# Attention's mixing matmuls in pairs of 33 columns on the two halves of TensorE's array, and three of four low halves on GpSimd

## The chip, the cores and the metric

The kernel runs on one core of a Trainium2 chip. The metric is the device time of one launch in microseconds (us). Matmuls run on TensorE (PE in the rows; PEld is its weight loads), elementwise work on VectorE (DVE), ScalarE (ACT) and GpSimd (POOL), and SyncE (SP) issues most DMAs. TensorE's granted clock has two levels, 1.2 and 2.4 GHz; 1.00 in a row is 2.4 GHz throughout.

## The reference

A decoder block with four gated parts, each added to the residual `x` (4 x 512 x 512): attention over a context, a ternary mixture of experts, a cross attention with 16 heads over 1024 keys, and an expert layer. The change lies in the third:

```python
Q = query @ Wq.T + bq                      # 4 x 512 x 512, 16 heads of 32
K = key_value @ Wk.T + bk                  # 4 x 1024 x 512
V = key_value @ Wv.T + bv
scores = jnp.einsum('bhsd,bhtd->bhst', Q, K) * scale
attn = jax.nn.softmax(scores, axis=-1)
ctx = jnp.einsum('bhst,bhtd->bhsd', attn, V)
x = x + jnp.tanh(g_xattn[1]) * (ctx @ Wo.T + bo)
```

## The kernel before, in words

All values are 32-bit in the reference; the kernel splits each matmul operand into a bf16 high half and a bf16 rest (the low half), and adds the products. The program is a row of phases: `context_phase`, `readout_phase`, `router_phase`, `mixture_phase`, `query_phase`, `attention_phase`, `output_phase`, `expert_phase`. Each engine has its own instruction list, written out by hand in order; semaphores tie them together.

`attention_phase` handles batch after batch (B = 4), in each 16 heads (h), in each four quarters of the 1024 keys (u). One (b, h, u) is a *step*, 256 in all. The scores stand transposed, 128 keys by 512 queries, two blocks (i = 0, 1) a step. TensorE does in the loop of a step (`batch`):

- `max_scores` (L1846): two full matmuls for the row maxima of the step 28 steps ahead (EARLY), into one of two `psM` buffers (`wait_free` waits until what lay there two places before has been used);
- `scores` (L1865): two matmuls for the step 4 ahead (AHEAD), into `psE`;
- `mix` (L1876): for each i the exponentials' high half `upper` (the upper 16 bits of each 32-bit word of `t_e`) and their low half (`t_low`) by the values, four matmuls of 96 columns (VW = 3 x 32: values high, values low, 32 columns of ones for the softmax sums), all into `psO[0:96]`, summed over u.

The other engines:

- ScalarE: `exponentials` (L1740), two per step for 4 steps ahead; `copy_out` (L1754) of `psO` to `ost` after each head; `max_copy` (L1748).
- VectorE: `halves` (L1786), the low half of an odd quarter, 128 x 1024 elements, 3 steps ahead; then `maximum` (L1778), the reduction of `psM`, 28 steps ahead. It also splits the output bias (`split_bias`, batch 1, heads 1 to 5) and inverts the sums (L1808, batch 3, head 5).
- GpSimd: `halves` (L1697) of the even quarters (`LO_ON_POOL = (0, 2)`, L1519), 4 ahead; before each it waits until VectorE has done its earlier ones (`lo_dve`). Once in 16 steps `max_parts` (L1707 to L1713) cuts the maxima of the next four heads into three bf16 parts, at step 5 of 16.
- At step 9 of 16 TensorE transposes these parts (`max_transpose`, L1854). The transpose takes one place in the ring of two `psM` buffers, so the maximum scores right behind it need the reduction of the step before, not of two steps before.
- SyncE: one DMA per head stores `ost` (L1674), and the loads of the next batch's keys, values (L1243) and queries.

The stage's order is thus fixed by the lists; 16 steps (four heads) make one *group*, from one transpose to the next. `output_phase` then loads the mixed values, divides and projects: 12 full matmuls (L2084) and one of 3 rows for the bias (L2087, the matmul of `bones` and `brows`) per tile. `query_phase` sets the ones in `kst` and `vst` (L1336, L1338).

Of the kernel before, what the change touches and what calls it, by code (L numbers as in the profile page):

```python
# [17 lines left out]
VW = 3 * HD  # L18
# [1212 lines left out]
KV_LOADS = 7  # L1231


def load_keys_values(sp, b, g, keys_dram, values_dram, kst, vst, kv_loaded):
# [8 lines left out]
    sp.dma_start(vst[:, g, :, 0:2 * P], v_v[bb, g].rearrange("o p c n -> p (o c) n")).then_inc(kv_loaded[g], 16)  # L1243
# [16 lines left out]
def query_phase(nc, place, gates, mixture_dram, w32, w_loaded, bq, queries_dram, ident, xres, woT, kst, vst, ones_set,  # L1260
# [6 lines left out]
    with ExitStack() as c:  # L1267
# [43 lines left out]
        with nc.Block() as block:  # L1311
            @block.gpsimd
            def _(pool):
# [18 lines left out]
                for b in range(B):  # L1332
                    if b >= 1:
                        deviations(b)
                    pool.wait_ge(rstd_ready, b + 1)
                    nc.gpsimd.memset(kst[3 * HD:, b, :, :], 1.0).then_inc(ones_set, 1)  # L1336
                    pool.wait_ge(ones_set, 2 * b + 1)
                    nc.gpsimd.memset(vst[:, b, :, 2 * P:], 1.0).then_inc(ones_set, 1)  # L1338
                    pool.wait_ge(ones_set, 2 * b + 2)
# [162 lines left out]
def load_sums(sp, b, target, mixed_dram, loaded):  # L1502

    sp.dma_start(target, mixed_dram.rearrange("b r (h d) s -> b r h d s", d=HD)[b, 2, :, 0, :]).then_inc(loaded, 16)


def attention_phase(nc, queries_dram, keys_dram, values_dram, mixed_dram, ident, qst, loaded, kst, vst, kv_loaded, ones_set, o):
# [11 lines left out]
    LO_ON_POOL = (0, 2)  # L1519
    NLD = 3  # L1520
    mixed_v = mixed_dram.rearrange("b r (h d) s -> b h r d s", h=NH)

    with ExitStack() as c:
# [8 lines left out]
        ost = sb("t_ost", [VW, 2, S], F32)  # L1532
# [16 lines left out]
        mixed = sem("t_mixed")  # L1549
# [77 lines left out]
        with nc.Block() as block:  # L1627
            @block.sync
            def _(sp):
# [10 lines left out]
                def prepare_output(h):  # L1640

                    if h == 2:
                        for i in range(2):
                            sp.wait_ge(stored[i], 16 * (LAST * NH // 2 + 1))
                        for b in range(LAST):
                            load_sums(sp, b, o.sums[b * NH:(b + 1) * NH, :], mixed_dram, o.sums_loaded)
# [13 lines left out]
                def batch(b):  # L1660
                    for h in range(NH):
# [18 lines left out]
                for i in range(2):  # L1680
                    sp.sem_inc(stored[i], 16)
# [3 lines left out]
                for i in range(2):  # L1685
                    sp.wait_ge(stored[i], 16 * (B * NH // 2 + 1))
# [47 lines left out]
            def _(act):  # L1734
# [15 lines left out]
                def copy_out(b, h):  # L1750
                    head = b * NH + h
                    act.wait_ge(mixed, head * 4 + 4 + RING)
                    act.wait_ge(stored[h % 2], b * 16 * (NH // 2) + h // 2 * 16 + 16)
                    nc.scalar.copy(ost[:, h % 2, :], psO[0:VW, h % 2, :]).then_inc(copied_out, 1)  # L1754

# [18 lines left out]
            def _(dve):  # L1774
# [13 lines left out]

                for m in range(EARLY):
# [13 lines left out]
                def prepare_output(b, h, u):  # L1803
                    if (b, u) == (1, 0) and 1 <= h < 6:
                        split_bias(h - 1)
                    if (b, h, u) == (LAST, 5, 0):
                        dve.wait_ge(o.sums_loaded, 16 * LAST)
# [29 lines left out]
            def _(pe):  # L1837
# [30 lines left out]
                def mix(b, h, u, i):  # L1868
                    head = b * NH + h
                    g = h // G  # L1870
                    if i == 0:
                        wait_lo(pe, head, u)
                        if u == 0:
                            pe.wait_ge(copied_out, head + 1)
                    for r, part in enumerate((upper(h, u), low[:, slot(h, u), :, :])):
                        last = nc.tensor.matmul(psO[0:VW, h % 2, :], vst[:, g, 2 * u + i, :].rearrange("p (w h) -> p h w", h=G)[:, h % G, :],  # L1876
                                                part[:, i, :], start=(u == 0 and i == 0 and r == 0),
                                                stop=(u == 3 and i == 1 and r == 1))
                    if i == 1:
                        last.then_inc(mixed, 1)  # L1880

                pe.wait_ge(ones_set, 2 * HG)
# [7 lines left out]
                def batch(b):  # L1890
                    for _, h, u in steps(b):
# [14 lines left out]
def output_phase(nc, mixed_dram, ident, woT, x3_dram, xeT, prefetch, o):  # L1906
# [596 lines left out]
```

## Time and profile before

| what | value |
|---|---|
| median of 3 runs | 1695.03 us (1694.34 to 1701.07) |
| the profiled execution | 1700.02 us, span 1698.3 us |
| mean granted clock | 0.933 |
| TensorE, VectorE, ScalarE, GpSimd busy | 86%, 74%, 57%, 25% of the span |
| first and last mixing matmul | 768.1 and 1237.2 us from the span's start |
| matmuls in attention | L1846, L1865 x512 each, L1876 x1024 |
| low halves | VectorE x128, GpSimd x128 |

The busy shares are means over phases with different limits. A matmul's length in a row (0.38 us) is longer than the spacing of two (0.22), since they are pipelined; the spacing is what counts. The page's 40 slices are 42.5 us each; attention fills slices 18 to 29.

### The profile page before, as it was taken

The numbers are of one execution on the slowest core, as the hardware profiler recorded it, in microseconds if no ns is written. First come the engines' busy times: TensorE is split into PE (matmuls) and PEld (weight loads), VectorE is DVE, ScalarE is ACT, GpSimd is POOL, SyncE is SP. The second block draws the span as 40 slices with busy tenths as digits, with TensorE's granted clock in tenths as the row PEclk, the third lists the DMA queues.
The fourth block names the chain that finished last, engine by engine and source line by source line (L and its number), as shares of the span: only waits on it lengthen the run. The fifth ranks groups of instructions, "written<-read, shape, count | busy, mean of one in ns | idle before, by whom it ended". The sixth has DMA issues, their size and how long they took to land. (4 is left out here: it accounts for less than half of the span.)

```text
span 1698.3 us, 23860 instructions
## 1 busy us (share of the span) xinstructions
PE 1454.6 (86%) x8551; PEld 833.1 (49%) x8551; DVE 1260.2 (74%) x1550; ACT 972.8 (57%) x1440; POOL 425.0 (25%) x335
## 2 busy tenths in 40 slices
PE   4989996999851975879999999999977699999996
PEld 3445453555430543315555555555523566666653
DVE  4788866678762878579999999999787676655651
ACT  5778733355441865407676676776823676665651
POOL 0122200000053006205555555555730000000000
PEclk9999998999965987869999999999989799999998
DMA  6789750000046439301334233244363786666640
GB/s 229 222 268 305 234 211 32 1 2 1 1 193 257 137 110 215 111 26 44 84 72 103 66 93 84 73 102 132 80 196 141 233 278 213 218 203 221 223 145 25
DMA packets 145830, 236.83 MB, mean 139 GB/s; under 512 B 11324, under 2 KB 61503, under 8 KB 144584
## 3 DMA queue, kind: packets, MB, share of 16 engines
q1 hardware_dynamic: 140232, 210.39, 40.4%
q0 software_dynamic: 5504, 25.20, 4.1%
q8 instruction: 56, 0.92, 0.2%
q14 instruction: 38, 0.31, 0.1%
HBM read 169.48 MB, written 59.59 MB: 135 GB/s over the span
## 5 line engine op out<-in xcount | busy, mean ns | idle before, releaser
L1740 ACT ACTIVATE t_e<-t_psE 128x512 f32<-128x512 f32 x512 | 304.7, 597 | 139.8 <-PE t_psE L1865 131.6
L1778 DVE TENSOR_REDUCE t_nmax<-t_psM 128x1 f32<-128x1024 f32 x256 | 301.6, 1210 | 14.7 <-PE t_psM L1846 14.6
L1697 POOL TENSOR_TENSOR t_low<-t_e 128x1024 bf16<-128x1024 f32 x128 | 250.1, 1956 | 201.1 <-ACT t_e L1740 179.3
L1876 PE MATMUL t_psO<-t_e,vst 128*96 128x512 bf16 x512 | 201.1, 393 | 2.5 <-POOL t_low L1697 2.5
L1865 PE MATMUL t_psE<-qst,kst 99*128 99x512 bf16 x512 | 195.6, 384 | 0.1
L1876 PE MATMUL t_psO<-t_low,vst 128*96 128x512 bf16 x512 | 193.6, 378 | 0.0
L1846 PE MATMUL t_psM<-kst,qst 96*128 96x512 bf16 x512 | 164.3, 405 | 31.6 <-DVE t_nmax L1778 26.4
L1786 DVE TENSOR_TENSOR t_low<-t_e 128x1024 bf16<-128x1024 f32 x128 | 175.7, 1373 | 17.8 <-ACT t_e L1740 17.3
L2334 PE MATMUL e_psG<-late_flat,e_w1p 128*128 (+1 forms) x1536 | 175.5, 278 | 12.8 <-DVE e_hT L2278 8.1
L2334 PEld LDWEIGHTS e_psG<-late_flat,e_w1p 128*128 128x128 bf16 x1536 | 152.9, 100 | 35.7 <-issue 8.3
L2349 PE MATMUL e_psO<-e_w2p,e_hT 128*128 128x512 bf16 x768 | 167.1, 379 | 0.0
L2349 PEld LDWEIGHTS e_psO<-e_w2p,e_hT 128*128 128x128 bf16 x768 | 75.1, 98 | 88.9
L1876 PEld LDWEIGHTS t_psO<-t_e,vst 128*96 128x96 bf16 x512 | 84.2, 165 | 65.1 <-POOL t_low L1697 6.0
L1876 PEld LDWEIGHTS t_psO<-t_low,vst 128*96 128x96 bf16 x512 | 84.5, 165 | 27.7 <-issue 0.4
L1846 PEld LDWEIGHTS t_psM<-kst,qst 96*128 96x128 bf16 x512 | 46.8, 99 | 99.5 <-DVE t_nmax L1778 53.3
L116 POOL DMA_DIRECT2D ternary<-c_wout x48 | 46.3, 964 | 180.9 <-ACT c_wout L228 180.9
L2230 ACT CAST e_w2p<-xres 128x2048 bf16<-128x2048 f32 x32 | 60.7, 1897 | 53.1 <-PE e_psO L2349 32.6
L2236 ACT ACTIVATE e_g<-e_psG,e_b1T 128x256 f32<-128x256 f32 x128 | 53.6, 470 | 64.8 <-PE e_psG L2334 40.3
L358 PE MATMUL c_psG<-ctxT,c_wT 128*128 128x512 bf16 x384 | 88.1, 381 | 0.0
L675 PE MATMUL a_psS<-ctxT,a_xT 128*128 128x512 bf16 x384 | 87.7, 386 | 0.0
L361 PE MATMUL c_psG<-c_wT,ctxT 128*128 128x512 bf16 x384 | 87.1, 379 | 0.0
L2270 DVE TENSOR_TENSOR e_w1p<-piece,e_w1p 128x2048 bf16<-128x2048 f32 x32 | 72.2, 2287 | 18.2 <-ACT e_w1p L2225 18.2
(258 smaller groups left out, 2312.8 us busy)
## 6 DMA issues: line engine op xcount, KB each, us to landing
piece<-in_L_ffn_w SPq DMA_DIRECT2D x32, 1024.0 KB, 13.8
xres<-in_L_ffn_w SPq DMA_DIRECT2D x32, 1024.0 KB, 14.7
wT<-ternary POOLq DMA_DIRECT2D x8, 1536.0 KB, 20.6
kst<-keys SPq DMA_DIRECT2D x96, 128.0 KB, 4.3
mixed<-t_ost SPq DMA_DIRECT2D x64, 192.0 KB
c_rows<-in_ctx SPq DMA_DIRECT2D x8, 1024.0 KB, 9.6
xres<-in_L_ffn_wg SPq DMA_DIRECT2D x8, 1024.0 KB, 7.6
xres<-in_L_ffn_wu SPq DMA_DIRECT2D x8, 1024.0 KB, 7.4
```

What stands on the lines that cost most here:

```text
L358: last = nc.tensor.matmul(psG[:, k, :], wT[:, 0, a, k * P:(k + 1) * P], ctxT[:, b, q * 512:(q + 1) * 512], start=(i == 0), stop=(i == 11))
L361: last = nc.tensor.matmul(psG[:, k, :], ctxT[:, a, q * 512 + k * P:q * 512 + (k + 1) * P], wT[:, 1, b, :], start=(i == 0), stop=(i == 11))
L675: last = nc.tensor.matmul(psS[:, par, h * 512:(h + 1) * 512], xT[:, par, ra * KC + k, :], ctxT[:, rb * KC + k, bass.ds(b * T + h * 512, 512)],
L1697: nc.gpsimd.tensor_tensor(low[:, slot(h, u), :, :], e32[:, slot(h, u), :, :], upper(h, u), ALU.subtract).then_inc(lo_pool, 1)
L1740: nc.scalar.activation(e32[:, slot(h, u), i, :], psE[:, i, :], ACT.Exp, scale=SC).then_inc(expd, 1)
L1778: nc.vector.tensor_reduce(nmax[:, h // G % 2, h % G, u:u + 1], banks_of(place_of_max(b, m)).rearrange("p a t -> p (a t)"), AX_X, ALU.max, ...
L1786: nc.vector.tensor_tensor(low[:, slot(h, u), :, :], e32[:, slot(h, u), :, :], upper(h, u), ALU.subtract).then_inc(lo_dve, 1)
L1846: last = nc.tensor.matmul(banks_of(place_of_max(b, m))[:, i, :], qst[0:KR, g, h % G, u * P:(u + 1) * P], kst[0:KR, g, h % G, i * 512:(i + ...
L1865: nc.tensor.matmul(psE[:, i, :], kst[:, g, h % G, k * P:(k + 1) * P], qst[:, g, h % G, :], start=True, stop=True).then_inc(scored, 1)
L1876: last = nc.tensor.matmul(psO[0:VW, h % 2, :], vst[:, g, 2 * u + i, :].rearrange("p (w h) -> p h w", h=G)[:, h % G, :], part[:, i, :], sta ...
L2334: last = nc.tensor.matmul(psG[:, g % 4, i, :], w1p[:, ra, k, f:f + P], xeT[:, rb * KC + k, ee, :].rearrange("p o s -> p (o s)"), start=(n ...
L2349: last = nc.tensor.matmul(psO[:, m, :], hT[:, ra, k, m * P:(m + 1) * P], w2p[:, rb, k, :], start=(k == 0 and i == 0), stop=(k == FC - 1 an ...
```

## The change

Mixing goes from four matmuls of 96 columns to six of 33 (VW = 33: 32 values and a column of ones or zeros). A step issues its two score matmuls together, then three pairs; the first of a pair writes `psO[0:33]`, the second `psO[64:97]` (SIDE = 64). The products are high by values high, low by values high, high by values low; low by values low is not formed. Both halves are copied out and stored, and the sums of both are added before the reciprocal. `LO_ON_POOL` becomes (0, 1, 2).

```diff
-VW = 3 * HD
+VW = HD + 1
...
-KV_LOADS = 7
+KV_LOADS = 8
...
-    sp.dma_start(vst[:, g, :, 0:2 * P], v_v[bb, g].rearrange("o p c n -> p (o c) n")).then_inc(kv_loaded[g], 16)
+    for r in range(2):
+        sp.dma_start(vst[:, g, :, r * VW * HG:r * VW * HG + P],
+                     v_v[bb, g].rearrange("o p c (r n) -> p (o c) r n", r=2)[:, :, r, :]).then_inc(kv_loaded[g], 16)
...
-                    nc.gpsimd.memset(vst[:, b, :, 2 * P:], 1.0).then_inc(ones_set, 1)
-                    pool.wait_ge(ones_set, 2 * b + 2)
+                    nc.gpsimd.memset(vst[:, b, :, P:P + HG], 1.0).then_inc(ones_set, 1)
+                    pool.wait_ge(ones_set, 3 * b + 2)
+                    nc.gpsimd.memset(vst[:, b, :, VW * HG + P:2 * VW * HG], 0.0).then_inc(ones_set, 1)
+                    pool.wait_ge(ones_set, 3 * b + 3)
...
-    LO_ON_POOL = (0, 2)
+    LO_ON_POOL = (0, 1, 2)
+    SIDE = P // 2
...
-        ost = sb("t_ost", [VW, 2, S], F32)
+        ost = sb("t_ost", [SIDE + VW, 2, S], F32)
+        sums_more = sb("t_sums_more", [(B - 1) * NH, S], F32)
...
-                        sp.dma_start(mixed_v[bass.ds(b, 1), h].rearrange("o r d s -> (o r) d s"),
-                                     ost[:, h % 2, :]).then_inc(stored[h % 2], 16)
+                        for r in range(2):
+                            rows = slice(r * SIDE, r * SIDE + HD)
+                            sp.dma_start(mixed_v[b, h, r], ost[rows, h % 2, :]).then_inc(stored[h % 2], 16)
+                            sp.dma_start(sums_v[b, h, r], ost[r * SIDE + HD:r * SIDE + VW, h % 2, :]).then_inc(stored[h % 2], 16)
...
-                    nc.scalar.copy(ost[:, h % 2, :], psO[0:VW, h % 2, :]).then_inc(copied_out, 1)
+                    nc.scalar.copy(ost[:, h % 2, :], psO[0:SIDE + VW, h % 2, :]).then_inc(copied_out, 1)
...
+                nc.vector.memset(psO[:, :, :], 0.0).then_inc(mix_cleared, 1)
...
+                        nc.vector.tensor_tensor(o.sums[:, :], o.sums[:, :], sums_more[:, :], ALU.add).then_inc(sums_added, 1)
+                        dve.wait_ge(sums_added, 1)
                         nc.vector.reciprocal(o.sums[:, :], o.sums[:, :]).then_inc(o.rsums_ready, 1)
...
-                def mix(b, h, u, i):
+                def mix(b, h, u):
...
+                    def values(i, r):
+                        return vst[:, g, 2 * u + i, r * VW * G:(r + 1) * VW * G].rearrange("p (w h) -> p h w", h=G)[:, h % G, :]
+
+                    def add(side, i, r, part, first=False, last=False):
+                        return nc.tensor.matmul(psO[side * SIDE:side * SIDE + VW, h % 2, :], values(i, r), part[:, i, :],
+                                                start=first, stop=last)
+
+                    if u == 0:
+                        pe.wait_ge(copied_out, head + 1)
+                    wait_lo(pe, head, u)
+                    add(0, 0, 0, high, first=u == 0)
+                    add(1, 0, 0, rest, first=u == 0)
+                    add(0, 1, 0, high)
+                    add(1, 1, 0, rest)
+                    add(0, 0, 1, high, last=u == 3)
+                    add(1, 1, 1, high, last=u == 3).then_inc(mixed, 1)
+
+                pe.wait_ge(ones_set, 3 * HG)
+                pe.wait_ge(mix_cleared, 1)
...
-                        for i in range(2):
-                            if within(b2, h2):
+                        if within(b2, h2):
+                            for i in range(2):
                                 scores(b2, h2, u2, i)
-                            mix(b, h, u, i)
+                        mix(b, h, u)
```

The output phase adds its two sums before its reciprocal in the same way.

TensorE's list, one step behind the first transpose. Before:

```order
L1854 MATMUL t_psM<-ident,t_nparts 128x128
L1846 MATMUL t_psM<-kst,qst 128x512 x2
L1865 MATMUL t_psE<-qst,kst 128x512
L1876 MATMUL t_psO<-t_e,vst 96x512
L1876 MATMUL t_psO<-t_low,vst 96x512
L1865 MATMUL t_psE<-qst,kst 128x512
```

And a step now:

```order
L1859 MATMUL t_psM<-kst,qst 128x512 x2
L1878 MATMUL t_psE<-qst,kst 128x512 x2
L1891 MATMUL t_psO<-t_e,vst 33x512
L1891 MATMUL t_psO<-t_low,vst 33x512
L1891 MATMUL t_psO<-t_e,vst 33x512
L1891 MATMUL t_psO<-t_low,vst 33x512
L1891 MATMUL t_psO<-t_e,vst 33x512 x2
```

Eight matmuls a step became ten, and the second score stands before the first mixing matmul.

VectorE's list in attention, low halves and reductions. Before:

```order
L1786 TENSOR_TENSOR t_low<-t_e 128x1024
L1778 TENSOR_REDUCE t_nmax<-t_psM 128x1 x2
L1786 TENSOR_TENSOR t_low<-t_e 128x1024
L1778 TENSOR_REDUCE t_nmax<-t_psM 128x1 x2
L1786 TENSOR_TENSOR t_low<-t_e 128x1024
```

And now:

```order
L1796 TENSOR_TENSOR t_low<-t_e 128x1024
L1788 TENSOR_REDUCE t_nmax<-t_psM 128x1 x4
L1796 TENSOR_TENSOR t_low<-t_e 128x1024
L1788 TENSOR_REDUCE t_nmax<-t_psM 128x1 x4
L1796 TENSOR_TENSOR t_low<-t_e 128x1024
```

One low half per four reductions, where there were two. On GpSimd a group's list goes from eight low halves between two `max_parts` to twelve:

```order
L1713 TENSOR_TENSOR t_nparts<-t_nrest,t_nparts 128x16
L1697 TENSOR_TENSOR t_low<-t_e 128x1024 x8
L1707 TENSOR_TENSOR t_nparts<-t_nmax,t_nparts 128x16
L1709 TENSOR_TENSOR t_nrest<-t_nmax,t_nparts 128x16
L1711 TENSOR_TENSOR t_nparts<-t_nrest,t_nparts 128x16
```

```order
L1723 TENSOR_TENSOR t_nparts<-t_nrest,t_nparts 128x16
L1707 TENSOR_TENSOR t_low<-t_e 128x1024 x12
L1717 TENSOR_TENSOR t_nparts<-t_nmax,t_nparts 128x16
L1719 TENSOR_TENSOR t_nrest<-t_nmax,t_nparts 128x16
L1721 TENSOR_TENSOR t_nparts<-t_nrest,t_nparts 128x16
```

The four operations of `max_parts` keep their place, behind quarter 1 of a head, which is now GpSimd's own.

## Rows read from the trace of the kernel before

**Rows 1.** Windows view, stretches between transposes; columns busy us and count per engine, clock.

```profile
1059.14:1088.82 29.68, 28.39 (x130) 16.72 (x129) 28.67 (x25) 21.15 (x37) 16.91 (x12) 1.00 0.35 85
903.70:936.40 32.70, 29.40 (x130) 16.25 (x129) 32.70 (x29) 21.03 (x38) 17.79 (x12) 1.00 0.33 78
1144.50:1177.80 33.30, 30.21 (x130) 17.01 (x129) 32.28 (x27) 21.27 (x38) 16.96 (x12) 0.95 0.46 155
784.20:1204.40 420.20, 398.57 (x1798) 232.62 (x1797) 404.76 (x339) 295.59 (x519) 237.64 (x168) 1.00 0.35 87
1204.40:1237.60 33.20, 30.71 (x132) 17.99 (x130) 21.70 (x12) 24.91 (x45) 27.64 (x11) 1.00 0.37 99
```

**Rows 2.** Timeline, one step; columns start, length, engine, line, operation, tiles, count, idle.

```profile
1081.63 0.60 PE L1846 MATMUL t_psM<-kst,qst 96*128 96x512 bf16 x2
1082.07 0.38 PE L1865 MATMUL t_psE<-qst,kst 99*128 99x512 bf16 x1
1082.29 0.39 PE L1876 MATMUL t_psO<-t_e,vst 128*96 128x512 bf16 x1
1082.52 0.38 PE L1876 MATMUL t_psO<-t_low,vst 128*96 128x512 bf16 x1
...
1083.39 0.38 PE L1846 MATMUL t_psM<-kst,qst 96*128 96x512 bf16 x1
...
1082.54 1.20 ACT L1740 ACTIVATE t_e<-t_psE 128x512 f32<-128x512 f32 x2 [0.56 <-PE t_psE L1865]
```

**Rows 3.** Timeline, around a transpose: TensorE, then VectorE, then GpSimd.

```profile
1085.15 0.22 PE L1854 MATMUL t_psM<-ident,t_nparts 128*128 128x128 bf16 x1
1086.66 0.61 PE L1846 MATMUL t_psM<-kst,qst 96*128 96x512 bf16 x2 [1.29 <-DVE t_nmax L1778]
...
1081.51 2.34 DVE L1778 TENSOR_REDUCE t_nmax<-t_psM 128x1 f32<-128x1024 f32 x2
1083.78 1.69 DVE L1786 TENSOR_TENSOR t_low<-t_e 128x1024 bf16<-128x1024 f32 x1
1085.40 1.21 DVE L1778 TENSOR_REDUCE t_nmax<-t_psM 128x1 f32<-128x1024 f32 x1
...
1080.46 1.20 POOL L1707 TENSOR_TENSOR t_nparts<-t_nmax,t_nparts 128x16 bf16<-128x16 f32 x1
```

**Rows 4.** Timeline, low halves: on a free port, then behind the other engine's.

```profile
1082.50 1.89 POOL L1697 TENSOR_TENSOR t_low<-t_e 128x1024 bf16<-128x1024 f32 x1
...
1088.82 1.23 DVE L1786 TENSOR_TENSOR t_low<-t_e 128x1024 bf16<-128x1024 f32 x1 [0.28 <-ACT t_e L1740]
...
1226.87 4.06 DVE L1786 TENSOR_TENSOR t_low<-t_e 128x1024 bf16<-128x1024 f32 x2 [1.87 <-ACT t_e L1740]
...
1220.99 7.61 POOL L1697 TENSOR_TENSOR t_low<-t_e 128x1024 bf16<-128x1024 f32 x3 [1.16 <-DVE t_low L1786]
1229.76 2.92 POOL L1697 TENSOR_TENSOR t_low<-t_e 128x1024 bf16<-128x1024 f32 x1 [1.16 <-DVE t_low L1786]
```

**Rows 5.** Timeline of TensorE in the output projection, the 3-row bias matmul.

```profile
1261.67 0.38 PE L2087 MATMUL o_psG<-late_flat 3*128 3x512 bf16 x1
1261.98 2.76 PE L2084 MATMUL o_psG<-late_flat,o_cpair 128*128 128x512 bf16 x12
1264.68 0.38 PE L2087 MATMUL o_psG<-late_flat 3*128 3x512 bf16 x1
```

**Rows 6.** Groups of the page, and the store's issue (ns min/median/max, first and last start).

```profile
L1778 DVE TENSOR_REDUCE t_nmax<-t_psM 128x1 f32<-128x1024 f32 x256 | 301.6, 1210 | 14.7 <-PE t_psM L1846 14.6
...
L1674 SPq DMA_DIRECT2D mixed<-t_ost x64: 666/667/2049, 776.2 to 1238.2; - x64
...
L1338 POOL MEMSET vst<- x4: 957/1036/1117, 661.1 to 697.9; 128x1024 bf16 x4
```

More of the change, by code:

```diff
@@ L1499, in load_rsums, with load_sums, attention_phase @@
                      rsum_v[b:b + 1, g].to_broadcast([HD, KC, S])).then_inc(loaded, 16)
-def load_sums(sp, b, target, mixed_dram, loaded):
-    sp.dma_start(target, mixed_dram.rearrange("b r (h d) s -> b r h d s", d=HD)[b, 2, :, 0, :]).then_inc(loaded, 16)
-def attention_phase(nc, queries_dram, keys_dram, values_dram, mixed_dram, ident, qst, loaded, kst, vst, kv_loaded, ones_set, o):
+def load_sums(sp, b, targets, sums_dram, loaded):
+    for r, target in enumerate(targets):
+        sp.dma_start(target, sums_dram[b, r]).then_inc(loaded, 16)
+def attention_phase(nc, queries_dram, keys_dram, values_dram, mixed_dram, sums_dram, ident, qst, loaded, kst, vst, kv_loaded, ones_set, o):
     SC = float(HD) ** -0.5
@@ L1643, in prepare_output @@
                         for i in range(2):
-                            sp.wait_ge(stored[i], 16 * (LAST * NH // 2 + 1))
+                            sp.wait_ge(stored[i], 64 * (LAST * NH // 2 + 1))
                         for b in range(LAST):
-                            load_sums(sp, b, o.sums[b * NH:(b + 1) * NH, :], mixed_dram, o.sums_loaded)
+                            load_sums(sp, b, [v[b * NH:(b + 1) * NH, :] for v in (o.sums, sums_more)], sums_dram, o.sums_loaded)
                         sp.wait_ge(o.brows_loaded, 16)
@@ L1680, in _ @@
                 for i in range(2):
-                    sp.sem_inc(stored[i], 16)
+                    sp.sem_inc(stored[i], 64)
                 put_max(0, 0)
@@ L1685, in _ @@
                 for i in range(2):
-                    sp.wait_ge(stored[i], 16 * (B * NH // 2 + 1))
+                    sp.wait_ge(stored[i], 64 * (B * NH // 2 + 1))
             @block.gpsimd
@@ L1866, in scores @@
                                      qst[:, g, h % G, :], start=True, stop=True).then_inc(scored, 1)
-                def mix(b, h, u, i):
+                def mix(b, h, u):
                     head = b * NH + h
                     g = h // G
[L1871 to L1882, printed above, removed]
+                    high, rest = upper(h, u), low[:, slot(h, u), :, :]
+                    def values(i, r):
[14 more added lines that the diff above has]
+                pe.wait_ge(mix_cleared, 1)
                 for m in range(EARLY):
@@ L2062, in _ @@
                 low(1)
-                dve.wait_ge(sums_loaded, 16)
-                nc.vector.reciprocal(sums[:, :], sums[:, :]).then_inc(rsums_ready, 1)
+                dve.wait_ge(sums_loaded, 32)
+                nc.vector.tensor_tensor(sums[:, 0, :], sums[:, 0, :], sums[:, 1, :], ALU.add).then_inc(sums_added, 1)
+                dve.wait_ge(sums_added, 1)
+                nc.vector.reciprocal(sums[:, 0, :], sums[:, 0, :]).then_inc(rsums_ready, 1)
                 for b in range(B):
@@ L2372, in flamingo_kernel @@
     queries_dram = dram("queries", (B, 2, D, S), BF16)
-    mixed_dram = dram("mixed", (B, 3, D, S), F32)
+    mixed_dram = dram("mixed", (B, 2, D, S), F32)
+    sums_dram = dram("sums", (B, 2, NH, S), F32)
     dispatch_dram = dram("dispatch", ((NT + E - 1) * P, DW // 2), F32)
```

25 lines of the change are left out of this document (13 added, 12 removed).

## The prediction

> **What bounds the kernel now.** The windows view comes first: the change touches attention, 470 of 1698 us, so only that stage counts. One group of the schedule is 16 steps (a step is one head's quarter of the keys) from one `max_transpose` to the next, and lasts 29.68 us, in which TensorE works 28.39 us and VectorE 28.67 us, both 96% at a granted clock of 1.00 (2.4 GHz); the 14 groups from the second transpose to the last take 420.20 us and the rest of the stage 33.20 us [rows 1]. So two engines are at their limit at once, and the timeline has to say which of them holds which step. It shows TensorE issuing without a gap: a step is eight matmuls, from 1081.63 to 1083.39, 1.76 us or 0.22 us each, the ones that read the high half (`t_e`, every second 16-bit word) 0.23 and the others 0.215 [rows 2]. 16 x 1.76 is 28.16 us. The missing 1.52 us is one place: the transpose itself takes 0.22 us, and it takes one of the two `psM` buffers, so the maximum scores behind it wait for the reduction of the step just before, and TensorE stands 1.29 us behind VectorE [rows 3]. VectorE is late there because its low half of quarter 3 stands in front of that reduction (from 1085.40) and took 1.69 us in place of 1.23 [rows 3, 4]. Thus 15 of 16 steps are bound by TensorE, one by the chain exp, low half, reduction.
>
> Why 1.69? A low half on VectorE and one on GpSimd do not run side by side. A VectorE one that starts on a free port takes 1.23 us and a GpSimd one 1.89; one that starts while the other engine's is under way ends about 1.08 us (VectorE) or 1.75 us (GpSimd) after the other has ended. The two VectorE ones from 1226.87 take 4.06 us together and end at 1230.93; the GpSimd one that starts at 1229.76, under the second of them, takes 2.92 and ends at 1232.68; the GpSimd one from 1082.50 ends at 1084.39, and VectorE's from 1083.78 at 1085.47 [rows 3, 4]. The low halves of both engines are therefore one queue.
>
> **The change, part by part.** *TensorE.* Per step it removes four mixing matmuls (96 columns) and adds six of 33 columns, in three pairs, one of each pair on the low and one on the high 64 columns of the array; the fourth product, low part by low values, goes. If a pair takes the time of one matmul, mixing costs 3 x 0.23 = 0.69 us in place of 0.89. The four full-width matmuls stay at 4 x 0.22 = 0.88. The gain of 0.2 us per step would be 51 us in 256 steps if nothing else came with it.
>
> Two things come with it. First, the array now changes shape twice in each step, full width to halves and back. The trace of before has such a change: the bias matmul of the output projection has 3 rows, which also uses a part of the array, between full matmuls. The next full one starts 0.31 us behind it and it starts 0.32 us behind the full one before, where neighbours of one shape are 0.216 apart (the 12 full ones last 2.76 us: 11 spacings and one length of 0.38). In sum, this one and the 12 behind it take 3.01 us, from 1261.67 to 1264.68; 13 x 0.216 is 2.81 [rows 5]. So a change of shape costs 0.10 us; twice a step 0.20. That is a change of rows and here it is columns; bounds are 0 (if the queue hides it) and 0.16, a matmul's 0.38 us from start to end less the 0.216 spacing. I take 0.10. The Trainium skill (TensorEngine Tiling (Array Packing), Key Properties) says that a change of tiling mode drains the engine. Read as a full drain that is the upper bound, and the sum would end at plus 42 us in place of plus 20; the row says that less than a drain is paid. Second, the second half's stream starts behind the first's: between 0 (both start at once) and 0.10 us (no more than a change of shape costs), I take the middle, 0.05, as no row is nearer to either end. TensorE's step is then 0.88 + 0.20 + 0.05 + 0.69 = **1.82 us**, 0.06 more than now; with the bounds 1.57 to 1.99.
>
> *Low halves.* VectorE keeps quarter 3 alone, GpSimd does 0, 1 and 2. VectorE's work per head falls from 4 x 1.14 + 2 x 1.2 = 7.0 to 4 x 1.14 + 1.2 = 5.8 us (two reductions in a row take 2.34, so one adds 1.14 [rows 3]), in a head of 7.3. The common queue grows: per head 3 x 1.85 + 1.09 = 6.64 us, against 2 x 1.85 + 2 x 1.2 = 6.1 before. At 1.82 us per step (7.28 per head) that still fits.
>
> *The transpose's stall.* Does it go? Follow one group with 1.82 us steps, counted from the start of step 5. The exps of a quarter end 0.29 us into the next step (scored 0.44 us into its own; 0.47 from the score's start to the first exp, 1.20 for both [rows 2]). GpSimd's quarter 0 runs from 0.29 to 2.18 and quarter 1 to 4.03; then `max_parts` stands in its queue, four small operations (2.04 us from 1080.46 to 1082.50 in the trace, the first of them 1.20 because VectorE had the port [rows 3]; some 1.1 us on a free port), to 5.1; then quarter 2 to 7.0. Step 8 starts at 5.46. VectorE's quarter 3 is ready at 5.75, gets the port at 7.0, ends at 8.1; its reduction ends at 9.27. TensorE wants the buffer at step 9 plus the transpose, 5.46 + 1.82 + 0.22 = 7.50, and gets it at 9.27. The stall is 1.77 us where it is 1.29 now [rows 3]: the relief of VectorE does not reach it, since the operation in front of the reduction is the same and the port is now held longer.
>
> A group becomes 16 x 1.82 + 0.22 + 1.77 = 31.1 us. The 14 groups: 14 x 31.1 + 0.3 (the reciprocal of batch 3, now behind an addition) = 435.7 against 420.2, **+15.5 us**. This includes what is regained: two groups in batch 1 (the bias is split on VectorE) and the one with the reciprocal are 32.70 and 33.30 us now [rows 1], as VectorE has no room; then it has room. In the stretch behind the last transpose, without maxima, the low halves bound both kernels: three GpSimd ones recur every 8.77 us (1220.99 to 1229.76), which is six steps, 1.46 us a step [rows 4]; after, 6.64 per four steps, 1.66. Some 20 steps: **+4 us**.
>
> *Small edits.* Clearing `psO` on VectorE before the first maximum, which TensorE waits for: between 0 and 1.2 us (a reduction of that size reads as long [rows 6]), +1. Four stores per head for one on SP's queue: the one takes 0.67 us to issue in heads of 7 us [rows 6]; four can be up to 2.7, hidden by the buffer of two heads, up to 1 us more behind the last head, but VectorE's quotients end there at the same time; 0 to 2, +0. In the query phase two tiny memsets replace one of 1.0 us on GpSimd [rows 6], outside the maxima's way, and the value loads are cut in two, issued more than a group ahead of need: 0. An addition of half a low half's columns, so some 0.6 us, before the last reciprocal in the output phase: 0.
>
> Sum +15.5 + 4 + 1 = **+20 us**. It is made against the profiled execution (1700.02 us, span 1698.3), which stands 5 us above the median; the forecast is laid on the median, 1695.0 + 20 = **1715 us**.
>
> **The rivals.** *The port queue is the bound and TensorE gets cheap (ends faster).* If a change of shape in columns costs nothing in the stream, the step is 1.57 to 1.62 us, 6.3 to 6.5 per head, less than the 6.64 of the low halves. Should VectorE's and GpSimd's low halves then fall into each other without extra waits, a group is 4 x 6.64 + 1.1 = 27.7 us and the transpose's stall lies inside it: 14 x 27.7 = 388, -32; with nothing at the end (its low halves also fall in step) and +1, about -31: 1664 us. It decides at a step of 1.66 us: only below it is TensorE no longer the bound. For it: TensorE pulls weight loads ahead everywhere in these rows. Against: the price of the change of rows [rows 5]. 0.15.
>
> *The same, but with the stall.* TensorE 1.57 to 1.75, GpSimd thrown late by `max_parts` in each group: the walk above with steps of 1.62 and 1.72 gives stalls of 2.57 and 2.17 and groups of 28.7 and 29.9 us, and what the low halves then wait for each other comes on top below 1.66. Taking 29.4 to 29.9: 14 groups are 8.6 to 1.6 us shorter than 420.2, with +4 and +1 that is -4 to +3, about 1694 us. 0.23.
>
> *A full drain.* Shape change 0.16: step 1.94 to 1.95, group 16 x 1.95 + 0.22 + 1.25 (the stall shrinks as the step grows, since steps 5 to 9 give GpSimd more time) = 32.7 us, 14 x 32.7 = 457.8, +37; with +4 and +1: 1737 us. 0.12.
>
> *The pairs do not overlap.* The change then doesn't do what it says: six matmuls in a row, 1.38 us; with 0.88 and 0.2 a step of 2.4 to 2.46; group 38.7 to 39.6: +121 to +134; behind the last transpose TensorE binds too, 20 x (1.96 - 1.46) = +10: about 1830 us. Nothing in the trace of before shows two matmuls at once, so nothing excludes it. The Trainium skill (TensorE: Matmul & The Clock Gate, Part 3: Packing small matmuls) gives 2.38x for three column tiles, so it speaks against this rival; no run here shows it yet. 0.10.
>
> **How the numbers follow.** Forecast (step 1.77 to 1.90; 1707 to 1727 us) 0.40, rivals 0.15, 0.23, 0.12, 0.10. What a measurement can tell from no change is 0.5%, 8.5 us: 1686.6 to 1703.5. Slower: 0.40 + 0.12 + 0.10, less a little for the forecast's low edge, 0.60. Faster: the first rival and the low edge of the second, 0.20. Same: 0.20. The range leaves out the pairs that do not overlap (0.10) and the far end of the faster rival (some 0.09): 1670 to 1750 us.
>
> **What would show it.** Right: L1859, the maximum scores, every 1.8 us; the first matmul of the mixing 0.3 us behind the score before it and so for the score behind; in a pair two starts less than 0.1 us apart; one idle of 1.5 to 2 us per group before L1859 with VectorE as releaser; GpSimd in attention near 80% busy. Wrong: a step under 1.7 us (shape changes are free) or over 2.2 (no overlap), or a group whose length is a multiple of the low halves' queue and TensorE idle before the mixing matmuls with GpSimd as releaser.

## The result, and the profile after

| | before | after |
|---|---|---|
| median of the runs | 1695.03 us | 1715.54 us (1714.54 to 1716.45, 3 runs) |
| ratio | | 1.0105, 95% interval 1.0082 to 1.0128 |
| span of the profiled execution | 1698.3 us | 1713.8 us |
| first to last mixing matmul | 768.1 to 1237.2 | 767.1 to 1251.7 |

The changed kernel is slower by about 1%. The two profiled executions differ by 15.5 us, less than the medians (20.5), because the profiled one of before was at the upper end of its runs, 5 us above its median; the later runs of the kernel before, taken beside the experiments, had medians of 1696.4 to 1697.5.

The groups of the page that answer to the ones spoken of, for the kernel after (line, engine, operation, tiles, count, busy us and mean ns, idle and releaser):

```profile
L1707 POOL TENSOR_TENSOR t_low<-t_e 128x1024 bf16<-128x1024 f32 x192 | 365.3, 1924 | 117.6 <-ACT t_e L1750 97.6
L1788 DVE TENSOR_REDUCE t_nmax<-t_psM 128x1 f32<-128x1024 f32 x256 | 306.6, 1217 | 57.9 <-PE t_psM L1859 57.9
...
L1891 PE MATMUL t_psO<-t_e,vst 128*33 128x512 bf16 x1024 | 224.1, 397 | 6.3 <-POOL t_low L1707 6.3
...
L1891 PE MATMUL t_psO<-t_low,vst 128*33 128x512 bf16 x512 | 159.9, 394 | 0.0
...
L1796 DVE TENSOR_TENSOR t_low<-t_e 128x1024 bf16<-128x1024 f32 x64 | 110.6, 1729 | 35.9 <-ACT t_e L1750 35.9
```

GpSimd makes 192 low halves, VectorE 64. Of the latter each now takes 1729 ns in the mean, though the operation alone takes 1.23 us: 62 of the 64 take more than 1.3 us, because they start while one of GpSimd's is under way.

The windows view of the kernel after, first one group from a transpose to the next, then the group with the reciprocal, the 14 groups and the stretch behind the last transpose (the same stretches of the kernel before are [rows 1]):

```profile
1029.72:1060.30 30.58, 28.61 (x163) 9.31 (x162) 25.98 (x21) 19.52 (x38) 23.24 (x16) 1.00 0.35 75
1152.04:1188.66 36.62, 30.93 (x164) 9.60 (x162) 31.64 (x24) 19.81 (x38) 23.69 (x16) 0.91 0.41 136
782.55:1215.98 433.43, 402.59 (x2246) 130.21 (x2245) 365.88 (x284) 273.45 (x519) 326.03 (x224) 0.99 0.35 76
1215.98:1251.70 35.72, 29.44 (x177) 9.68 (x177) 14.45 (x6) 22.85 (x44) 34.48 (x16) 1.00 0.35 82
```

A group is 30.58 us for 29.68. VectorE's busy time in it went from 28.67 to 25.98 us and gained nothing; GpSimd's went from 16.91 to 23.24. The 14 groups take 433.43 us for 420.20 and the end 35.72 for 33.20.

One step on TensorE, the timeline of the kernel after (before: [rows 2]):

```profile
1057.72 0.42 PE L1891 MATMUL t_psO<-t_e,vst 128*33 128x512 bf16 x1
1057.73 0.62 PE L1891 MATMUL t_psO<-t_low,vst 128*33 128x512 bf16 x2
1057.98 0.61 PE L1891 MATMUL t_psO<-t_e,vst 128*33 128x512 bf16 x3
1058.53 0.61 PE L1859 MATMUL t_psM<-kst,qst 96*128 96x512 bf16 x2
1058.97 0.60 PE L1878 MATMUL t_psE<-qst,kst 99*128 99x512 bf16 x2
1059.50 0.42 PE L1891 MATMUL t_psO<-t_e,vst 128*33 128x512 bf16 x1
```

From 1057.72 to 1059.50 is 1.78 us in these rounded rows, 1.772 in the mean (1.76 before). The first `t_e` and the first `t_low` start within 0.01 us of each other: the pairs run side by side, and the six matmuls, with the change of shape behind them, take the 0.80 us to 1058.53. Of the step mixing is 0.80 us, the four full matmuls 0.88, and 0.09 lies between the last score and the first mixing matmul beyond the usual 0.216.

The transpose's stall in the timeline of the kernel after, TensorE, VectorE, GpSimd (before: [rows 3]):

```profile
1060.30 0.23 PE L1867 MATMUL t_psM<-ident,t_nparts 128*128 128x128 bf16 x1
1062.51 0.61 PE L1859 MATMUL t_psM<-kst,qst 96*128 96x512 bf16 x2 [1.97 <-DVE t_nmax L1788]
...
1058.79 2.52 DVE L1796 TENSOR_TENSOR t_low<-t_e 128x1024 bf16<-128x1024 f32 x1 [0.17 <-ACT t_e L1750]
1061.24 1.21 DVE L1788 TENSOR_REDUCE t_nmax<-t_psM 128x1 f32<-128x1024 f32 x1
...
1057.29 0.22 POOL L1717 TENSOR_TENSOR t_nparts<-t_nmax,t_nparts 128x16 bf16<-128x16 f32 x1
...
1058.34 1.89 POOL L1707 TENSOR_TENSOR t_low<-t_e 128x1024 bf16<-128x1024 f32 x1
```

TensorE is idle for 1.97 us where it was 1.29. VectorE's low half of quarter 3 starts at 1058.79, 0.45 us behind GpSimd's of quarter 2, which `max_parts` had made late; it ends at 1061.31, 1.08 us behind GpSimd's end, and the reduction that TensorE waits for stands behind it. So of the 0.90 us that a group grew, the stall is 0.69 and the 16 steps together are 0.21.

### The profile page after: what moved, and what is told of

Same layout as the page of the kernel before. It is cut to its first block and busy times, and to the rows that moved or that the text cites. A ratio compares the mean times of both kernels' runs of the same rounds, so it can differ in the third digit from the quotient of the medians.

```text
span 1713.8 us, 25090 instructions
## 1 busy us (share of the span) xinstructions
PE 1453.6 (85%) x8987; PEld 718.2 (42%) x9063; DVE 1212.2 (71%) x1489; ACT 947.5 (55%) x1440; POOL 520.1 (30%) x403
## 5 line engine op out<-in xcount | busy, mean ns | idle before, releaser
L1707 POOL TENSOR_TENSOR t_low<-t_e 128x1024 bf16<-128x1024 f32 x192 | 365.3, 1924 | 117.6 <-ACT t_e L1750 97.6
L1750 ACT ACTIVATE t_e<-t_psE 128x512 f32<-128x512 f32 x512 | 277.9, 595 | 178.2 <-PE t_psE L1878 178.1
L1788 DVE TENSOR_REDUCE t_nmax<-t_psM 128x1 f32<-128x1024 f32 x256 | 306.6, 1217 | 57.9 <-PE t_psM L1859 57.9
L1891 PE MATMUL t_psO<-t_e,vst 128*33 128x512 bf16 x1024 | 224.1, 397 | 6.3 <-POOL t_low L1707 6.3
L1891 PE MATMUL t_psO<-t_low,vst 128*33 128x512 bf16 x512 | 159.9, 394 | 0.0
L1878 PE MATMUL t_psE<-qst,kst 99*128 99x512 bf16 x512 | 157.1, 386 | 0.2
L1796 DVE TENSOR_TENSOR t_low<-t_e 128x1024 bf16<-128x1024 f32 x64 | 110.6, 1729 | 35.9 <-ACT t_e L1750 35.9
L1891 PEld LDWEIGHTS t_psO<-t_e,vst 128*33 128x33 bf16 x1024 | 67.6, 113 | 138.7 <-issue 56.9
L1859 PEld LDWEIGHTS t_psM<-kst,qst 96*128 96x128 bf16 x512 | 30.7, 100 | 158.3 <-issue 99.2
L2303 DVE TENSOR_TENSOR e_hT<-e_g,e_hT 128x512 bf16<-128x512 f32 x64 | 43.7, 690 | 55.5 <-ACT e_hT L2264 55.5
```

What stands on the lines that cost most here:

```text
L1707: nc.gpsimd.tensor_tensor(low[:, slot(h, u), :, :], e32[:, slot(h, u), :, :], upper(h, u), ALU.subtract).then_inc(lo_pool, 1)
L1750: nc.scalar.activation(e32[:, slot(h, u), i, :], psE[:, i, :], ACT.Exp, scale=SC).then_inc(expd, 1)
L1788: nc.vector.tensor_reduce(nmax[:, h // G % 2, h % G, u:u + 1], banks_of(place_of_max(b, m)).rearrange("p a t -> p (a t)"), AX_X, ALU.max, ...
L1796: nc.vector.tensor_tensor(low[:, slot(h, u), :, :], e32[:, slot(h, u), :, :], upper(h, u), ALU.subtract).then_inc(lo_dve, 1)
L1859: last = nc.tensor.matmul(banks_of(place_of_max(b, m))[:, i, :], qst[0:KR, g, h % G, u * P:(u + 1) * P], kst[0:KR, g, h % G, i * 512:(i + ...
L1878: nc.tensor.matmul(psE[:, i, :], kst[:, g, h % G, k * P:(k + 1) * P], qst[:, g, h % G, :], start=True, stop=True).then_inc(scored, 1)
```

## Where the low halves run: two experiments

**The changed kernel with two on GpSimd.**

```diff
-    LO_ON_POOL = (0, 1, 2)
+    LO_ON_POOL = (0, 2)
```

> The changed kernel, but with two low halves of four on GpSimd (quarters 0 and 2) as before. Theory A (the step is bound by TensorE at 1.77 us, eleven hundredths of it won by pairing and given back by two shape changes of 0.09 us; what is lost on top is a longer stall behind the transpose, since three low halves on GpSimd push quarter 2 late and hold the port): the group falls from 30.58 to about 29.5 us and the whole to about 1706 us, 9 us less than the change. Rival B (all of the loss is in TensorE's new stream and the extra stores; where the low halves run is free): within 2 us of 1715. Rival C (the third low half on GpSimd is the whole loss): 1695 or less.

Measured: 1702.23 us, ratio to before 1.0027 (1.0013 to 1.0042). A group in the windows view:

```profile
1022.65:1052.36 29.71, 28.60 (x163) 9.29 (x161) 28.78 (x25) 19.53 (x38) 16.91 (x12) 1.00 0.39 77
```

29.71 us: the group of the kernel before, to 0.03 us, and 0.87 less than with three. So of the roughly 20 us some 13 come from the third low half. That is more than theory A's 9: besides the ordinary group, the fall of the clock in the first group is gone (29.75 us for 32.11), and the stretch from the last transpose to the last mixing matmul is 4.3 us shorter (31.8 us for 36.1). Pairing as such left the ordinary group as long as it was, but only in sum: its 16 steps are 0.2 us longer than those of the kernel before, and its stall is shorter by the same (1.11 us for 1.29). The 5 us that are left against before lie outside the ordinary groups: 1.7 in the group with the reciprocal (35.03 us for 33.29), of which the rest of attention gives about half back, and the others outside attention, since from the first transpose to the end of the last mixing matmul the two profiles take 482.3 and 481.4 us. What lies behind that matmul takes 465.0 and 460.7 us in the two profiles. It took 463.8 in another version whose code there is that of the kernel before (the one with the transpose at step 8, below), so most of this difference may be scatter between executions.

**The kernel before with three on GpSimd.**

```diff
-    LO_ON_POOL = (0, 2)
+    LO_ON_POOL = (0, 1, 2)
```

> The kernel before, with only the third low half moved to GpSimd. Theory A: the stall behind the transpose grows by 0.9 us in each group (29.68 to 30.5), 1695 + 9 = 1704 us. Rival B: 1695 or a little less, as VectorE is relieved. Rival C: about 1715.

Measured: 1718.82 us, ratio 1.0120 (1.0095 to 1.0144), 20 to 22 us and not 9. Of the fifteen intervals between transposes eight are 30.54 to 31.7 us, as expected, but four are 32.0 to 32.2. One of these, TensorE then VectorE in the timeline, and last a windows row from the stall's end on:

```profile
1032.48 0.22 PE L1854 MATMUL t_psM<-ident,t_nparts 128*128 128x128 bf16 x1
1034.85 1.03 PE L1846 MATMUL t_psM<-kst,qst 96*128 96x512 bf16 x2 [2.15 <-DVE t_nmax L1778]
1035.68 0.63 PE L1865 MATMUL t_psE<-qst,kst 99*128 99x512 bf16 x1
...
1031.10 2.56 DVE L1786 TENSOR_TENSOR t_low<-t_e 128x1024 bf16<-128x1024 f32 x1 [0.28 <-ACT t_e L1740]
...
1034.70:1038.10 3.40, 3.25 (x8) 1.38 (x9) 1.32 (x2) 1.07 (x2) 0.93 (x1) 0.51 0.17 39
```

After 2.15 us of idle time the matmuls follow each other every 0.43 us: the granted clock is 0.51 (1.2 GHz) for 3.4 us, which costs 1.5 us more. Nine other stalls of 2.00 to 2.16 us in this run kept the clock at 1.00. The group's growth is theory A's (0.86 us), but it comes in thirteen groups, 11 us; the four falls of the clock, 6 us, were in nobody's sum, and neither was the stretch behind the last transpose, 36.5 us for 33.2, where the low halves are the bound; the last interval adds 1.5, and some 4 us come back where VectorE was full before. Rival C's 1715 is the nearer total, but for these other reasons.

## What a change of shape and a pair cost

**Four changes of shape a step.**

```diff
-                def mix(b, h, u):
+                def mix(b, h, u, between):
...
                     add(1, 0, 0, rest, first=u == 0)
+                    between()
                     add(0, 1, 0, high)
...
-                            for i in range(2):
-                                scores(b2, h2, u2, i)
-                        mix(b, h, u)
+                            scores(b2, h2, u2, 0)
+                        mix(b, h, u, lambda: within(b2, h2) and scores(b2, h2, u2, 1))
```

`between` issues the second score matmul of the step.

> The changed kernel with the second score matmul of a step put behind the first pair, so that TensorE changes shape four times a step and not twice; same instructions. Theory A: each change costs 0.09 us, the step goes from 1.77 to 1.94 us, the group from 30.58 to 32.3 us (the stall shrinks by some 0.9), 1715 + 26 = 1741 us. A full drain at each change would make it 0.16 each: 1715 + 50 = 1765. If the 0.09 belongs to something else (the semaphore wait ahead of the mixing), no change: 1715.

Measured: 1752.54 us, ratio 1.0316 (1.0289 to 1.0343). TensorE's timeline, a step from 1060.93:

```profile
1060.93 0.60 PE L1859 MATMUL t_psM<-kst,qst 96*128 96x512 bf16 x2
1061.37 0.38 PE L1878 MATMUL t_psE<-qst,kst 99*128 99x512 bf16 x1
1061.68 0.42 PE L1891 MATMUL t_psO<-t_e,vst 128*33 128x512 bf16 x1
1062.03 0.39 PE L1878 MATMUL t_psE<-qst,kst 99*128 99x512 bf16 x1
```

From a score to the pair behind it 0.31 us, from the pair to the score behind it 0.35. The step is 2.00 us for 1.77, so two more changes cost 0.23, 0.11 each; the group is 33.34 us, its stall 1.11 for 1.97. It is the shape that costs, more than theory A's 0.09 (hence 1752 us for its 1741) and less than 0.16, the prediction's bound for a full drain. The Trainium skill (TensorEngine Tiling (Array Packing), Key Properties) says that the engine drains at a change of mode; the traces show a cost of 0.09 to 0.12 us each time.

**The two halves in turn.**

```diff
                     add(0, 0, 0, high, first=u == 0)
-                    add(1, 0, 0, rest, first=u == 0)
                     add(0, 1, 0, high)
-                    add(1, 1, 0, rest)
                     add(0, 0, 1, high, last=u == 3)
+                    add(1, 0, 0, rest, first=u == 0)
+                    add(1, 1, 0, rest)
                     add(1, 1, 1, high, last=u == 3).then_inc(mixed, 1)
```

> The changed kernel with the three matmuls of the low columns first and the three of the high columns behind them; same instructions. Theory A: matmuls overlap only with a neighbour on the other half, so five spacings of 0.22 and one pair: mixing from 0.80 to about 1.25 us, the step 2.2 us, 1715 + 100 to 110 us = 1820. Rival: the array keeps a stream of its own for each half and lets it run ahead, then nothing changes: 1715.

Measured: 1718.71 us, one run. Theory A was wrong here and its rival right; the 3 us above the change are two more falls of the clock behind the transpose in this execution (three such stalls and not one, 1.5 us each). TensorE's timeline:

```profile
1040.90 0.42 PE L1891 MATMUL t_psO<-t_e,vst 128*33 128x512 bf16 x1
1040.91 0.62 PE L1891 MATMUL t_psO<-t_low,vst 128*33 128x512 bf16 x2
1041.16 0.61 PE L1891 MATMUL t_psO<-t_e,vst 128*33 128x512 bf16 x3
1041.71 0.39 PE L1859 MATMUL t_psM<-kst,qst 96*128 96x512 bf16 x1
```

The first `t_low`, fourth in the program's order, starts 0.01 us behind the first `t_e`, and mixing still takes 0.80 us (1040.90 to 1041.71). The order in which the two halves' matmuls stand does not matter; that they stand alternately in the change is no part of its effect.

**All six on one half.**

```diff
-                    add(1, 0, 0, rest, first=u == 0)
-                    add(0, 1, 0, high)
-                    add(1, 1, 0, rest)
-                    add(0, 0, 1, high, last=u == 3)
-                    add(1, 1, 1, high, last=u == 3).then_inc(mixed, 1)
+                    add(0, 0, 0, rest)
+                    add(0, 1, 0, high)
+                    add(0, 1, 0, rest)
+                    add(0, 0, 1, high)
+                    add(0, 1, 1, high, last=u == 3).then_inc(mixed, 1)
```

> The changed kernel with all six mixing matmuls of a step on the low 64 columns (into psO[0:33], the high rows stay zero); the same number of matmuls, weight loads and shape changes, and the same sum. Theory A: what the pairs win is the running side by side on the two halves; on one half six spacings of 0.22 us follow each other, the step is 2.4 us, the group about 38.9, and the whole 1715 + 130 = 1845 us. Rival (33 columns are quicker than 96 by themselves, or the queue hides part of it): under 1800.

Measured: 1836.28 us. TensorE's timeline, the six of one step:

```profile
1059.85 0.42 PE L1891 MATMUL t_psO<-t_e,vst 128*33 128x512 bf16 x1
1060.10 0.38 PE L1891 MATMUL t_psO<-t_low,vst 128*33 128x512 bf16 x1
1060.32 0.39 PE L1891 MATMUL t_psO<-t_e,vst 128*33 128x512 bf16 x1
1060.54 0.38 PE L1891 MATMUL t_psO<-t_low,vst 128*33 128x512 bf16 x1
```

They follow each other every 0.22 us; the step is 2.42 and the group 38.83 us. So 33 columns are no quicker than 96, and the pair is worth 0.65 us a step: without it the change would have cost 140 us. With it mixing costs three spacings for four, 0.2 us less, and the two changes of shape take the same 0.2 back. The stalls behind the transpose are gone in this run, since the step leaves VectorE and GpSimd time enough. The group is theory A's (38.9), the total 9 us below its 1845.

## Taking the stall away

**The transpose one step earlier, both kernels.** At step 9 the maximum scores wait for the reduction of step 8, and VectorE's list has the low half of quarter 3 in front of that one. At step 8 they wait for step 7's, which has none in front.

```diff
-        LATE = 5
-        SPLIT_AT, TURN_AT = 5, GROUP + LATE + GROUP - EARLY
+        LATE = 4
+        SPLIT_AT, TURN_AT = 4, GROUP + LATE + GROUP - EARLY
```

> The changed kernel with the transpose of the maxima's parts one step earlier (LATE = 4, so at step 8 of 16, and max_parts at step 4). The maximum scores behind it then wait for a reduction that no low half stands in front of. Theory A (15 of 16 steps at 1.77 us, and the rest of the group is the transpose's stall): the group falls from 30.58 to 28.9 us, 15 groups 25 us, minus 0 to 3 for the two falls of the clock that are gone: about 1692 us. Rival (GpSimd, with 12 low halves and max_parts in a group, is the bound, and the stall only shows it): the wait moves to the mixing matmuls and the group stays above 30, 1710 us or more.

> The kernel before with the same move of the transpose. Theory A: the group falls from 29.68 to 28.64 us (16 x 1.76, the transpose, and a quarter of a microsecond), 1695 - 12 = 1683 us. Rival (VectorE, 96% busy, is the bound of the group in the kernel before): no change, 1695.

Measured, the changed kernel: 1690.85 us, ratio to before 0.9964 (0.9943 to 0.9985), a group of 28.8 us:

```profile
1014.58:1043.38 28.80, 28.59 (x163) 9.31 (x161) 26.06 (x21) 19.40 (x38) 23.20 (x17) 1.00 0.40 80
```

The kernel before: 1688.59 us, ratio 0.9956 (0.9940 to 0.9972), a group of 28.68 us, the transpose and the scores behind it, and the windows row:

```profile
1018.88 0.22 PE L1854 MATMUL t_psM<-ident,t_nparts 128*128 128x128 bf16 x1
1019.39 0.39 PE L1846 MATMUL t_psM<-kst,qst 96*128 96x512 bf16 x1 [0.29 <-DVE t_nmax L1778]
...
1018.88:1047.56 28.68, 28.39 (x130) 16.74 (x129) 28.60 (x25) 21.14 (x38) 16.90 (x13) 1.00 0.36 88
```

Both groups come out within 0.1 us of theory A's, and so does the total of the changed kernel (1692). The kernel before gained 8 us and not its 12: attention did become 12.1 us shorter in the profile (469.3 us for 481.4 from the first transpose to the last mixing matmul), but what lies behind it, whose code is the same, was 3.1 us longer (463.8 for 460.7), which no run explains. The same two numbers are worth some 25 us in the changed kernel and 8 in the one before, and with them the two kernels differ by 2 us where they differed by 20: so the stall was the larger part of what the change cost, GpSimd with its 23.2 us of work is not the bound, and VectorE, 28.60 us of 28.68 busy, just keeps pace in the one before.

**Three on GpSimd with the transpose at step 8, without pairs.** As the last one, with `LO_ON_POOL = (0, 1, 2)` and `SPLIT_AT` 3.

> The kernel before with three low halves on GpSimd and the transpose one step earlier (LATE = 4, max_parts at step 3). Theory A: the third low half costs only through the stall; without the stall the relief of VectorE pays where it was full (bias split, reciprocal): the group is 28.3 to 28.6 us, 1678 us. Rival (the port queue costs by itself): 1690 or more.

Measured: 1686.60 us, ratio 0.9930 (0.9908 to 0.9951).

```profile
1012.33 0.22 PE L1854 MATMUL t_psM<-ident,t_nparts 128*128 128x128 bf16 x1
1012.48 0.60 PE L1846 MATMUL t_psM<-kst,qst 96*128 96x512 bf16 x2
...
1012.33:1040.65 28.32, 28.32 (x130) 16.71 (x129) 25.34 (x21) 21.13 (x38) 24.07 (x17) 1.00 0.37 88
```

TensorE is busy for all of the 28.32 us. The third low half on GpSimd, which lost some 20 us with the transpose at step 9, now takes 0.35 us off a group. In the whole time that is about 2 us, which cannot be told from none (the intervals of the two ratios overlap), and the total is 9 us above theory A's 1678. Part of these are in the trace: behind the last transpose the third low half costs 5.6 us (38.8 us for 33.2 up to the last mixing matmul), since there the low halves are the bound.

And the pairs do not win: with three on GpSimd and the transpose at step 8 the group is 28.81 us with pairs and 28.33 without. Of this 0.48 us the steps are 0.21 (1.773 us for 1.760). The rest is a stall that the version with pairs still has, two steps behind the transpose:

```profile
1018.56 0.60 PE L1859 MATMUL t_psM<-kst,qst 96*128 96x512 bf16 x2 [0.21 <-DVE t_nmax L1788]
```

The two versions also differ in `SPLIT_AT` (4 and 3), and no run separates that from the pairs.

## The group with the reciprocal

In the kernel after, the timeline of VectorE in that group, then TensorE behind the stall, then the windows row of that stretch:

```profile
1176.55 1.79 DVE L1819 TENSOR_TENSOR late_flat<-late_flat,t_sums_more 48x512 f32<-48x512 f32 x1
1178.37 3.35 DVE L1821 RECIPROCAL late_flat<-late_flat 48x512 f32<-48x512 f32 x1
1181.64 3.51 DVE L1788 TENSOR_REDUCE t_nmax<-t_psM 128x1 f32<-128x1024 f32 x3
...
1182.86 1.03 PE L1859 MATMUL t_psM<-kst,qst 96*128 96x512 bf16 x2 [3.71 <-DVE t_nmax L1788]
...
1182.90:1187.00 4.10, 4.10 (x13) 1.06 (x14) 3.47 (x3) 1.67 (x3) 0.10 (x1) 0.50 0.00 0
```

The addition took 1.79 us and the reciprocal 3.35; TensorE was idle for 3.71 us and then ran at 0.50 of its clock, for 6.8 us in all. GpSimd's low half in front of the addition:

```profile
1175.90 4.19 POOL L1707 TENSOR_TENSOR t_low<-t_e 128x1024 bf16<-128x1024 f32 x2 [1.49 <-ACT t_e L1750]
```

The first of the two is under way when the addition starts, and the second waits for the addition: without it the two take 3.74 us. The kernel before has a fall of the clock in this group as well (0.95 over the group [rows 1]), but one of 3.4 us.

**Without the addition.**

```diff
-                        nc.vector.tensor_tensor(o.sums[:, :], o.sums[:, :], sums_more[:, :], ALU.add).then_inc(sums_added, 1)
-                        dve.wait_ge(sums_added, 1)
```

> The changed kernel without the addition of the second half's softmax sums ahead of the first reciprocal, so the first three batches are divided by the sums of one half alone. The group with the reciprocal took 36.61 us in the changed kernel where the others take 30.58. Theory A: VectorE's 5.1 us of addition and reciprocal in a row stop TensorE for 3.7 us and the granted clock falls to 1.2 GHz for 6.8 us; without the 1.8 us of the addition the stop is under 2.5 us and the low clock at most half as long, the group is 33 us and the whole about 3 us less, 1712. Rival (the reciprocal alone is enough): the group stays above 35.5.

Measured: 1715.48 us; the group is 33.98 us for 36.61. VectorE and TensorE:

```profile
1176.55 3.33 DVE L1819 RECIPROCAL late_flat<-late_flat 48x512 f32<-48x512 f32 x1
1179.81 3.51 DVE L1788 TENSOR_REDUCE t_nmax<-t_psM 128x1 f32<-128x1024 f32 x3
...
1181.02 1.04 PE L1857 MATMUL t_psM<-kst,qst 96*128 96x512 bf16 x2 [1.87 <-DVE t_nmax L1788]
```

The stop is 1.87 us and the matmuls behind it are still at the low clock, but for 3.4 us in place of 6.8. So the addition costs 2.6 us here, theory A's mechanism with a smaller gain in the group than its 33 us. The whole did not move (1712 was expected), but that is one run, and a gain of this size is within what runs scatter.

**The reciprocal in four pieces**, in the version with three on GpSimd and the transpose at step 8:

```diff
-                    if (b, h, u) == (LAST, 5, 0):
-                        dve.wait_ge(o.sums_loaded, 16 * LAST)
-                        nc.vector.reciprocal(o.sums[:, :], o.sums[:, :]).then_inc(o.rsums_ready, 1)
+                    if (b, h) == (LAST, 5):
+                        if u == 0:
+                            dve.wait_ge(o.sums_loaded, 16 * LAST)
+                        piece = o.sums[:, u * P:(u + 1) * P]
+                        nc.vector.reciprocal(piece, piece).then_inc(o.rsums_ready, 1)
...
-                        sp.wait_ge(o.rsums_ready, 1)
+                        sp.wait_ge(o.rsums_ready, 4)
```

> The kernel before with three low halves on GpSimd, the transpose at step 8, and the reciprocal of the sums of three batches cut into four pieces of 128 columns, one a step, in place of one of 3.3 us. Theory A: the 30.9 us group of the reciprocal falls to 28.6 and the clock no longer falls in it: 2 us less than the uncut one's 1686.6, so 1684 us, 0.7 to 0.9% under the kernel before. Rival: the pieces disturb four steps in place of one and give nothing, 1686.6.

Measured: 1685.60 us, ratio 0.9928 (0.9906 to 0.9949). The group fell from 30.89 to 28.33 us, as long as its neighbours, and the clock stays at 1.00 in all of attention. But a piece now stands in front of the reduction that TensorE waits for at the transpose behind this group, and there the stall is back:

```profile
1158.38 0.61 PE L1848 MATMUL t_psM<-kst,qst 96*128 96x512 bf16 x2 [1.62 <-DVE t_nmax L1778]
```

The interval behind it is 28.33 us for 27.76, so the two together gain 2.0 us. In the whole time that cannot be told from no change. This version has the lowest median of the study, 0.7% under the kernel before, though not clear of the one with the reciprocal in one piece.

## Why the prediction was right, step by step

- *TensorE bound in 15 of 16 steps, one chain in the sixteenth.* Right. With the measured step and stall, both kernels' groups follow from it within 0.1 us, and moving the transpose took the stall out of both.
- *A pair takes the time of one matmul.* Right: 0.65 us a step between pairs and one half.
- *A change of shape costs 0.10 us.* Right in size: 0.09 on the way in, 0.11 each in the run with four. The row of the 3-row matmul [rows 5] was a good measure, though it changes rows and the kernel changes columns. The full drain is out.
- *The second stream starts 0.05 us late.* Wrong: the two matmuls of a pair start 0.00 to 0.02 us apart. The step was 1.77 us and not 1.82, so it stands 0.01 above before and not 0.06. Most of the forecast loss per step was not there: the prediction put 0.96 us of a group's growth on the steps and 0.48 on the stall, and the trace has 0.21 and 0.69.
- *The stall grows to 1.77 us.* Right in kind, low in size: 1.97. The walk had the buffer free 9.27 us after the start of step 5; in the trace step 5 starts at 1053.21 and the scores at 1062.51, 9.30 us later. TensorE only stood there sooner, since its steps are shorter than was assumed: the walk with steps of 1.77 us gives 1.97.
- *14 groups, +15.5.* They gave +13.2, as the sum of misses that cancel in part: the ordinary group was 30.58 and not 31.1 (eleven groups, -4.7 in all); the last of the fourteen is short in both kernels, 27.3 us now, and I had given it 31.1 (-3.8); the group with the reciprocal was 36.62 (+5) and the first 32.1 (+1).
- *With the reciprocal VectorE has room, +0.3.* Wrong. I took the addition for small (0.6 us by its columns in the output phase, 0.3 here with the rest of the group); it started under one of GpSimd's low halves, took 1.79 us, and with the reciprocal behind it held three reductions back. The fall of the clock came on top, and the first group's extra 1.5 us is one too (0.55 between 784.6 and 788.4 us).
- *The end, +4.* Right in kind: TensorE waits there for GpSimd's low halves, and the stretch gave +2.5. *Clearing `psO`, +1*: it took 0.91 us ahead of the first maximum, and no trace shows that it cost anything (the first transpose and the first mixing matmul come 1 us sooner than before). *The stores*: 0.30 and 0.28 us to issue, two of each a head, 1.2 us in heads of 7: nothing waited.

That the time came out at 1715.5 us for a forecast of 1715 is in part luck. The terms +15.5, +4 and +1 measured +13.2, +2.5 and nothing, so the traces show some 16 us of the 20. The other 5 are the distance of the profiled execution of before from its median; against the later medians of the kernel before the change costs 18 to 19 us. What was right by its mechanism is the direction, TensorE as the bound of the steps, and the stall that the relief of VectorE does not reach.

The rivals: pairs that do not overlap and a full drain are excluded by the runs. The low halves' queue is not the bound of the groups in either form, since the groups at step 8 are TensorE's own sum to 0.3 us; it is the bound only behind the last transpose.

Open are whether the 4 us or so behind attention, between the changed kernel with two low halves on GpSimd and the kernel before, are more than scatter, and what decides whether a stall of about 2 us takes the clock down.

## What to carry to other kernels

Two engines at 96% busy need not be the bound together: find the one place in a period where the chain crosses from one to the other, and move that crossing before giving an engine less work; here one constant was worth more than the new matmul scheme, and decided whether moving work to GpSimd cost 20 us or nothing. Packing narrow matmuls into halves of the array works, but each change between full width and halves costs half a matmul here, which three pairs in place of four full matmuls just pay for; by these numbers the gain needs more pairs between two changes, which no run tried. When work moves to an engine that shares a port, add the two engines' work up as one queue, and look at who starts first.

## What the runs showed that was not expected

- A stall of about 2 us can be followed by 3.4 us at half of TensorE's clock, which costs 1.5 us: after four of thirteen stalls of 2.00 to 2.16 us in the kernel before with three low halves on GpSimd, one of thirteen of 1.96 to 1.98 us in the changed kernel, and three of thirteen in the one with the halves in turn, 1.96 us each.
- The two column halves take their matmuls from the list as two streams: three for one half followed by three for the other run as alternating ones do, at 1.776 us a step for 1.773.
- A two-input operation on VectorE or GpSimd that finds the port taken by the other's stands until that one ends: VectorE's low halves range from 1225 to 2523 ns in the changed kernel.
